# Transformer layer with a mixture of experts on 8 cores: the projection and rope of the next head pair are placed ahead of the attention of this one

## The reference, cut to what matters

```python
q = (x @ Wq + bq).reshape(b, s, h, hd)
k = (x @ Wk + bk).reshape(b, s, h, hd)
v = (x @ Wv + bv).reshape(b, s, h, hd)
q = _apply_rope(q, sin, cos)
k = _apply_rope(k, sin, cos)
scores = jnp.einsum('bqhd,bkhd->bhqk', q, k) * scale
scores = scores + jnp.where(causal, 0.0, -10000.0)
attn = jax.nn.softmax(scores, axis=-1)
ctx = jnp.einsum('bhqk,bkhd->bqhd', attn, v).reshape(b, s, h * hd)
x = _layernorm(x + ctx @ Wo + bo)
out = silu(x @ Ws1 + bs1) @ Ws2 + bs2
for e in range(8):
    out = out + w[e][:, None] * (silu(x @ We1[e] + be1[e]) @ We2[e] + be2[e])
x = _layernorm(x + out)
```

## Time and profile before

| What | Value |
|---|---|
| timed runs, us | 6355.78, 6049.62, 6242.84 (median 6242.84) |
| profiled execution, us | 6052.25 |
| its span on the slowest core (5) | 6050.5 |
| spans of the eight cores | 6037.8 to 6050.5 |
| mean granted TensorE clock of the cores | 0.921 to 0.924 |
| busy in the span: PE, DVE, ACT, POOL | 4939.9, 949.8, 1332.4, 834.5 us |

### The profile page before, as it was taken

How to read it: one execution, slowest core, us unless ns; L and a number is a source line. 1 busy time by engine, 2 the same in 40 slices (tenths; PEclk the granted TensorE clock), 3 DMA queues, 4 the chain that set the end, 5 groups by cost and what they waited for, 6 DMA issues and landing times. The chain is left out here.

```text
span 6050.5 us, 59935 instructions; the slowest of 8 cores (6037.8 to 6050.5 us)
## 1 busy us (share of the span) xinstructions
PE 4939.9 (82%) x22422; PEld 2136.8 (35%) x22422; DVE 949.8 (16%) x1192; ACT 1332.4 (22%) x1680; POOL 834.5 (14%) x717
## 2 busy tenths in 40 slices
PE   0065555555556999999999999999999999999996
PEld 0031111111123444444444444444444444444443
DVE  0012222222232101101101101101101101101104
ACT  0003333333343121121121121121121121121122
POOL 0001111111100000202212201201201201201201
PEclk9987777777777999999999999999999999999997
DMA  9949999999121101101101001001001001001001
GB/s 126 118 76 113 113 109 114 111 112 111 20 54 36 49 28 42 42 29 45 40 31 50 33 35 49 29 35 49 28 35 49 29 35 49 29 35 49 29 35 63
DMA packets 40122, 342.63 MB, mean 57 GB/s; under 512 B 5592, under 2 KB 6041, under 8 KB 16546
## 3 DMA queue, kind: packets, MB, share of 16 engines
q0 software_dynamic: 10368, 159.92, 23.4%
q1 hardware_dynamic: 29474, 178.88, 8.1%
HBM read 490.31 MB, written 159.38 MB: 107 GB/s over the span
## 5 line engine op out<-in xcount | busy, mean ns | idle before, releaser
L864 PE MATMUL pE<-x2bf,w1s 128*128 128x512 bf16 x9216 | 2010.2, 381 | 5.9 <-DMA w1s<-w1bf 5.9
L893 PE MATMUL pE<-h1bf,w2s 128*128 128x512 bf16 x9216 | 1992.0, 379 | 19.8 <-ACT h1bf L875 19.8
L875 ACT ACTIVATE h1bf<-pE,b_sb 128x512 bf16<-128x512 f32 x1152 | 791.9, 687 | 3153.7 <-PE pE L864 3153.7
L864 PEld LDWEIGHTS pE<-x2bf,w1s 128*128 128x128 bf16 x9216 | 905.5, 98 | 1108.0 <-issue 32.8
L893 PEld LDWEIGHTS pE<-h1bf,w2s 128*128 128x128 bf16 x9216 | 900.5, 98 | 1111.3 <-issue 28.1
L925 POOL TENSOR_TENSOR x<-x,tmp 128x512 f32<-128x512 f32 x512 | 647.8, 1265 | 3471.9 <-DVE tmp L916 3471.9
L487 ACT ACTIVATE et<-pS,cst 128x1024 bf16<-128x1024 f32 x320 | 385.4, 1204 | 778.6 <-PE pS L480 629.8
L916 DVE SCALAR_TENSOR_TENSOR tmp<-pE,b_sb,wb 128x512 f32<-128x512 f32 x256 | 192.2, 751 | 1586.5 <-PE pE L893 1586.5
L916 DVE SCALAR_TENSOR_TENSOR tmp<-pE,wb 128x512 f32<-128x512 f32 x256 | 177.1, 692 | 1618.5 <-PE pE L893 1618.5
L247 PE MATMUL pX<-identf_s,xstage 128*128 128x128 f32 x128 | 29.9, 414 | 344.5 <-DMA xstage<-x 340.8
L355 PE MATMUL pS<-xbf,wq 128*128 128x512 bf16 x256 | 71.3, 448 | 237.8 <-DMA wk<-wkr 237.8
(11 more groups left out here) (124 smaller groups left out, 1464.4 us busy)
## 6 DMA issues: line engine op xcount, KB each, us to landing
w1bf<-w1r POOLq DMA_DIRECT2D x18, 4096.0 KB, 160.3
w2bf<-w2r POOLq DMA_DIRECT2D x18, 4096.0 KB, 198.2
w1s<-w1bf SPq DMA_DIRECT2D x72, 1024.0 KB, 6.9
w2s<-w2bf SPq DMA_DIRECT2D x72, 1024.0 KB, 7.7
xstage<-x SPq DMA_DIRECT2D x16, 512.0 KB, 4.0
xres<-x SPq DMA_DIRECT2D x16, 512.0 KB, 3.8
y<-ybuf SPq DMA_DIRECT2D x16, 512.0 KB, 2.6
wv_sb<-wv POOLq DMA_DIRECT2D x8, 256.0 KB, 17.1
```

The lines of the kernel that those rows point to most:

```text
L864: e.matmul(o, l, r, start=st, stop=sp),
L875: e.activation(out=o, in_=i, func=AF.Silu, bias=b), inc=tA)
L893: e.matmul(o, l, r, start=st, stop=sp),
```

## The change

The body of the loop over chunks is split into two functions, `emit_projrope(j)` (loads, projection, rope) and `emit_attention(j)`. The loop calls them one chunk apart. q_sb, k_sb, qr_sb and kr_sb exist twice and are used by the chunk's parity. The evacuation goes from DVE (`tensor_scalar_add`) to ACT (`activation` with Identity and the bias). The weight slots are released behind the last matmul of their projection, and the waits on the shared buffers refer to the chunk before last.

```diff
@@ projection, rope
-        q_sb = ph.enter_context(nc.sbuf_tensor("q_sb", [128, S], BF16))
+        q_sb = [ph.enter_context(nc.sbuf_tensor(f"q_sb{i}", [128, S], BF16)) for i in range(2)]
...
-        for j in range(NCH):
+        def emit_projrope(j):
+            par = j % 2
             wqs, wqi, qtok = wq_ring.load("gpsimd", d["wqr"][j].rearrange("p k c -> p (k c)"))
             wks, wki, ktok = wk_ring.load("gpsimd", d["wkr"][j].rearrange("p k c -> p (k c)"))
             if j + 2 < NE:
                 precast_expert(j + 2)
             wq_ring.wait_loaded("tensor", qtok)
             wk_ring.wait_loaded("tensor", ktok)
...
-                    p.wait("vector", tT, mm)
-                    if j > 0 and g == 0:
-                        p.wait("vector", tG, prev_rope_done)
-                    ev = p.op("vector",
+                    if g == 3:
+                        wri[0].release(wri[1], tT, mm)
+                    p.wait("scalar", tT, mm)
+                    if g == 0 and j >= 2:
+                        p.wait("scalar", tG, rope_done[j - 2])
+                    ev = p.op("scalar",
                               lambda e, o=src[:, g * 512:(g + 1) * 512], i=slot[:, :],
                               b=bias_sb[:, j:j + 1]:
-                              e.tensor_scalar_add(o, i, b),
-                              inc=tV)
+                              e.activation(out=o, in_=i, func=AF.Identity, bias=b),
+                              inc=tA)
...
-                    if j > 0 and g == 0:
-                        p.wait("gpsimd", tT, prev_scores_done)
-                    p.wait("gpsimd", tV, evac_ticks[(nm, g)])
+                    if g == 0 and j >= 2:
+                        p.wait("gpsimd", tT, scores_done[j - 2])
+                    p.wait("gpsimd", tA, evac_ticks[(nm, g)])
...
-            prev_rope_done = p.c(tG)
-            p.wait("tensor", tG, prev_rope_done)
-
+            rope_done[j] = p.c(tG)
+
+        def emit_attention(j):
+            par = j % 2
             hA, hB = 2 * j, 2 * j + 1
+            krb, qrb = kr_sb[par], qr_sb[par]
+            p.wait("tensor", tG, rope_done[j])
...
             emit_norm(pend_norm)
-            pend_norm = None
-            prev_scores_done = p.c(tT)
-            wq_ring.release(wqi, tT, prev_scores_done)
-            wk_ring.release(wki, tT, prev_scores_done)
+            scores_done[j] = p.c(tT)
+
+        emit_projrope(0)
+        for j in range(NCH):
+            if j + 1 < NCH:
+                emit_projrope(j + 1)
+            emit_attention(j)
```

More of the change, by code:

```diff
@@ L306, in build_nc @@
         wk_sb = [ph.enter_context(nc.sbuf_tensor(f"wk{i}", [128, 1024], BF16)) for i in range(2)]
-        q_sb = ph.enter_context(nc.sbuf_tensor("q_sb", [128, S], BF16))
-        k_sb = ph.enter_context(nc.sbuf_tensor("k_sb", [128, S], BF16))
-        qr_sb = ph.enter_context(nc.sbuf_tensor("qr_sb", [128, S], BF16))
-        kr_sb = ph.enter_context(nc.sbuf_tensor("kr_sb", [128, S], BF16))
+        q_sb = [ph.enter_context(nc.sbuf_tensor(f"q_sb{i}", [128, S], BF16)) for i in range(2)]
+        k_sb = [ph.enter_context(nc.sbuf_tensor(f"k_sb{i}", [128, S], BF16)) for i in range(2)]
+        qr_sb = [ph.enter_context(nc.sbuf_tensor(f"qr_sb{i}", [128, S], BF16)) for i in range(2)]
+        kr_sb = [ph.enter_context(nc.sbuf_tensor(f"kr_sb{i}", [128, S], BF16)) for i in range(2)]
         t1f = [ph.enter_context(nc.sbuf_tensor(f"t1f{i}", [128, 512], F32)) for i in range(2)]
@@ L331, in build_nc @@
         rb_ring = Ring(p, recipb)
-        prev_rope_done = 0
-        prev_scores_done = 0
-        for j in range(NCH):
+        rope_done = {}
+        scores_done = {}
+        state = {"recip_busy": 0}
+        def emit_projrope(j):
+            par = j % 2
             wqs, wqi, qtok = wq_ring.load("gpsimd", d["wqr"][j].rearrange("p k c -> p (k c)"))
@@ L343, in build_nc @@
             evac_ticks = {}
-            for (nm, wsb, src, dst, bias_sb) in (
-                    ("q", wqs, q_sb, qr_sb, bq_sb), ("k", wks, k_sb, kr_sb, bk_sb)):
+            for (nm, wsb, wri, src, dst, bias_sb) in (
+                    ("q", wqs, (wq_ring, wqi), q_sb[par], qr_sb[par], bq_sb),
+                    ("k", wks, (wk_ring, wki), k_sb[par], kr_sb[par], bk_sb)):
                 for g in range(4):
@@ L357, in build_nc @@
                     mm = p.c(tT)
-                    p.wait("vector", tT, mm)
-                    if j > 0 and g == 0:
-                        p.wait("vector", tG, prev_rope_done)
-                    ev = p.op("vector",
+                    if g == 3:
[4 more added lines that the diff above has]
+                    ev = p.op("scalar",
                               lambda e, o=src[:, g * 512:(g + 1) * 512], i=slot[:, :],
                               b=bias_sb[:, j:j + 1]:
-                              e.tensor_scalar_add(o, i, b),
-                              inc=tV)
+                              e.activation(out=o, in_=i, func=AF.Identity, bias=b),
+                              inc=tA)
                     evac_ticks[(nm, g)] = ev
-                    ps_ring.release(si, tV, ev)
+                    ps_ring.release(si, tA, ev)
                 for g in range(4):
@@ L370, in build_nc @@
                     slot = slot[:, 0:512]
-                    p.wait("tensor", tV, evac_ticks[(nm, g)])
+                    p.wait("tensor", tA, evac_ticks[(nm, g)])
                     rt = p.op("tensor",
@@ L431, in emit_norm @@
             def emit_norm(pn):
-                nonlocal recip_busy
                 p.wait("tensor", tV, pn["rc"])
@@ L437, in emit_norm @@
                           inc=tT)
-                recip_busy = bt
+                state["recip_busy"] = bt
                 rslot, rbi = rb_ring.acquire("vector")
@@ L453, in build_nc @@
             pend_norm = None
-            recip_busy = 0
+            sm = 0
             for qh in range(2):
@@ L468, in build_nc @@
                                  lambda e, o=sslot[:, c0:c0 + 512],
-                                 l=kr_sb[r0:r0 + 64, kt * 128:(kt + 1) * 128],
-                                 r=qr_sb[r0:r0 + 64, win0:win0 + 512],
+                                 l=krb[r0:r0 + 64, kt * 128:(kt + 1) * 128],
+                                 r=qrb[r0:r0 + 64, win0:win0 + 512],
                                  sp=(off < 0):
@@ L501, in build_nc @@
                     p.wait("vector", tT, sm)
-                    p.wait("vector", tT, recip_busy)
+                    p.wait("vector", tT, state["recip_busy"])
                     p.op("vector", lambda e, i=smslot[0:1, :]:
```

## The result

The changed kernel is slower: the ratio of its runs to those of the kernel before is 1.0127, with a 95% interval of 1.0072 to 1.0182. Its median over ten runs is 6136.27 us (lowest 6129.99). The lowest of the kernel before is 6049.62 us, with its profiled execution at 6052.25; its median over ten runs, 6185.75 us, holds several executions in which the cores of a die ran at a lower clock, so a comparison of medians would show a gain that is not there. The profiled execution of the changed kernel took 6140.96 us (span 6139.3), 88.7 us more than the profiled execution before. So the loss is 77 us by the ratio, 80.4 us by the lowest times and 88.7 us by the two profiled executions; the ratio's interval, 44 to 110 us, holds all three.

A forecast was written before the change was run, and what follows sets the result against it. The prediction took POOL's transfer queue, 155.4 us a round, to bound the attention stage. Its terms, 90.0 − 6.2 − 0.8 = +83.0 us on 6052.25 us, gave 6135 us; range 6100 to 6335 us.

The forecast's parts named there:

- from the sum to a run's time: Run spread, a median 190.6 us above the profiled execution, carries over to any kernel; range drawn up to 6335 us.
- What bounds the kernel: Attention stage: POOL's queue of casts and weights gives the 155.4 us rounds; PE waits for the weights' landing.
- The order on PE: End of the attention stage: attention 6 now also stands behind the landing of weights 7, +90.0 us.
- the handover: Between the tail's two attentions: adds no term, as its waits are inside the 90.05 us of an attention.
- The rope's wait and the evacuation: Tail: attention 6 no longer waits for rope 7, −6.2 us; evacuation moved from DVE to ACT, −0.8 us.
- what is late next: First score tiles of attention 6: a pS slot, freed by DVE's evacuation of the last permutation matmuls, itself held by POOL.
- The table load: ACT: no extra function table loads from alternating Identity and Exp, taken as 0, with +2.6 us kept as an end.
- The landing of weights 7: Last weights of the attention stage: land at 1533.7 us, as before, a term of 0.
- behind the stage: Output stage after the attention stage's barrier: the delay goes on in full, nobody there gains by coming later.
- The idle stretches of PE: PE's waits for weights: about 129 us at projection 1, near 38 us at 2 to 7, some 360 us in all.
- A: Rival: the removed rope wait comes off each of 8 rounds, 65.2 us, giving 5987 us; chance 0.03.
- B: Rival: the tail's two attentions run at TensorE's low level, +68 us on the sum, 6203 us; chance 0.06.

The follow-up runs named there:

- three: Kernel before with a light queue: no cast in chunk 0, half an expert in chunks 1 to 6, experts 5 to 8 cast during the experts' stage; ratio 0.9945.
- four: Changed kernel with a light queue: no cast in chunk 0, half an expert in chunks 1 to 6, experts 5 to 8 cast during the experts' stage; ratio 0.9838.
- experiment one: Changed kernel with its loop back in the old order (projection j, attention j), all else kept; ratio to the kernel before 0.9997.
- two: Changed kernel with only the last projection (chunk 7) put back behind attention 6; ratio to the kernel before 1.0079.
- five: Changed kernel with the cast of expert 8 moved behind the weights of chunk 7 in POOL's queue; ratio to the kernel before 1.0068.
- six: Changed kernel, weights issued early, expert 2's cast added to the first block, two or three quarters per chunk (last none), expert 8's cast behind wo loads; ratio 0.9959.
- eight: From six: no casts in the first block or beside wo loads, three quarters per chunk (last two), 13 quarters during the experts' stage; ratio 0.9287.

## The prediction point by point: what held and what failed

The mechanism held, and two steps of the prediction failed. The first is the one from the sum to a run's time: "The sum explains none of that spread, which carries over to any kernel's runs". On this the range was drawn up to 6335 us, for a median 191 us above the profiled execution. It did not carry over: the median of the changed kernel's ten runs is 6136.27 us, 4.7 us below its profiled execution, and only one of the ten lies above 6202 us. Nor is it a trait of the kernel before, whose median was 193 us above its lowest time over three runs, 136 us over ten, and 11, 8 and 6 us in the three later series. Set beside that first median, 6242.84 us, the forecast of 6135 us would even read as a gain; the kernels' difference has to be taken from 6050 us. The second is a term put at nothing, "Weights 7 thus land at 1533.7 us, as before": that landing came 6.4 us later, the largest error among the terms of the sum. The terms one by one:

**What bounds the kernel** held throughout. The intervals stayed at 155.8 us and the queue at 99.0%, and taking casts out of the queue (three and four) brought the stage near PE's own pace.

**The order on PE**: +90.0 us was forecast. In the trace attention 7 follows attention 6 at 1655.34 us (the end of its broadcast) and ends at 1744.28: 88.9 us. An attention that starts behind another is 1.1 us shorter than one that starts behind a rope; I had said that the handover adds nothing, and it takes a little off. Attention 6, from its second pair of scores, took 88.7 us, against the 88.5 of attention 7 before.

**The rope's wait and the evacuation**: −6.2 and −0.8 us. From the first projection matmul to the second pair of scores there were 34.3 us before (1533.73 to 1568.02) and are 26.6 now (1540.08 to 1566.64): −7.7 where −7.0 was said. The name of what is late next was right: the waits at both pairs are on DVE's L385, and L385 itself waits for POOL. The table load stayed at one for the stage, so that Identity and Exp are served by one set here. The rule that I had quoted for it (the Trainium skill, ScalarE: Activation LUTs, "Table sets: the hidden batching unit") holds in this trace.

**The landing of weights 7**: forecast as unmoved, it came at 1540.08 instead of 1533.73, +6.4 us. The stage's first matmul was 1.5 us later (448.3, it was 446.8), before anything of the change could tell. The next six rounds took 156.1 us each where they had taken 155.7, 2.6 us in all, and the seventh 155.3 (from 1384.79) where it had taken 153.1 (from 1380.66 us, below), 2.2 us. The kernel before had thus had a short last round, and I took its end as the landing of both kernels.

```profile
1380.66 9.05 PE L355 MATMUL pS<-xbf,wq 128*128 128x512 bf16 x32 [34.48 <-DMA wk<-wkr]
```

The sum of the parts up to the stage's end is 6.4 − 7.7 + 0.2 + 88.9 = 87.8 us, and the profiled executions differ by 88.7. I had +83.0: the difference is this landing and 1.0 us behind the stage, less 1.6 that the other terms gave. Whether the later landing belongs to the change is not shown. Rounds still longer, 156.9 us, went with a ratio of 0.9997 in experiment one, but there the kernel before was some 14 us slower too, and the order was the old one. The difference of 80.4 us between the lowest times, below the sum, would fit chance in these two executions.

**The idle stretches of PE**: 129 us were forecast at projection 1 and 38 at the later ones; 130.75 and 38.4 to 41.1 are in the trace, and 378.8 in all where "some 360" was said. Of the difference 8.4 us are the wait ahead of projection 0, which the forecast had not counted.

**The rivals.** A, that every chunk would gain its wait of 8 us, describes the kernel where compute sets the pace, and there it came true in kind: the new order is ahead by 65, 61 and 39 us by the ratios of the three pairs with another queue, and the stage is 56, 41 and 44 us shorter in their traces, where A had 65.2. Here it did not decide. B, two attentions at TensorE's low level, did not occur: in windows over the two attentions of the tail the granted clock was 0.76 and 0.77, as in the earlier trace rows.

```profile
1563.90:1655.40 91.50, 65.66 (x282) 16.04 (x282) 31.65 (x15) 48.18 (x40) 6.16 (x6) 0.76 0.00 0
1655.40:1744.20 88.80, 64.56 (x280) 15.83 (x278) 32.34 (x16) 48.18 (x40) 0.00 (x0) 0.77 0.00 1
```

**What I had not seen**, though it did not enter the sum: that the landing of weights 6, with all that stands behind it, is only 38 us less late than landing 7 in the changed kernel (experiments two and five), and that the first block of 440 us is held by the same casts (six and eight).

## What to carry to other kernels

When work is moved ahead of other work on an in-order engine, look for the waits on transfers that move with it: to place the next round's work ahead pays only where its data are there already, and otherwise it lays work that could run behind an unfinished load. The end of a stage is the latest of all landings, each with everything that stands behind it on the engine, so count that sum for the last two or three landings and not only for the last. And where a large background transfer shares a queue, or merely the engines of the DMA, with small loads that somebody waits for, try each stage and measure it. Here it cost nothing that shows in the attention stage once the weights were issued a round ahead (PE waited for none in eight), 11 us a transfer beside the experts' loads, and about its whole length in the first block.

## What the runs showed that I had not expected

- A 4 MB cast beside a stage's loads costs that stage very different amounts. In the first block, one more expert (four casts) made it 153 us longer (594 us where it was 441), as much as the four casts themselves take, and taking both experts out brought the block down to 150 us. In the experts' stage 16 casts cost 181 us of waiting and 13 cost 138 us, 11 us each, against the 38 us for which one occupies the queue.
- The first block's length had looked like one of loading x; it was that of casts whose results nobody there needs. Moving the casts and issuing the weights early was worth ten times what the order was worth: 0.9352 without the new order, 0.9287 with it.
- The DMA pace of the same 17.3 MB per round was 155.4, 155.8 and 156.9 us in three profiles of kernels with the same queue. A few microseconds at a landing after seven rounds are no proof of an effect of the change.
